# Expert tiles of a one-core MoE kernel: gate and up projections computed in turned form, with the weights staged by a VectorE copy

## The reference

```python
scores = sigmoid(h @ gate_w.T)                  # 32 experts, grouped choice, 8 of them per token
g = silu(einsum('th,eih->tei', h, w_gate))      # I = 128, H = 256
u = einsum('th,eih->tei', h, w_up)
routed = einsum('tei,ehi->th', g * u * combine[:, :, None], w_down)
shared = silu(h @ sh_gate.T) * (h @ sh_up.T) @ sh_down.T
out = x + routed + shared
```

## Time and profile before

| | |
|---|---|
| time, median of 3 runs (lowest to highest) | 616.68 us (615.47 to 618.01) |
| span of the profiled execution | 615.6 us |
| PE busy | 563.7 us (92%) |
| DVE busy | 411.4 us (67%) |
| ACT busy | 372.2 us (60%) |
| POOL busy | 363.9 us (59%) |

### The profile page before, as it was taken

The page is one execution under the profiler, slowest core; times in us unless marked ns, Lnnn a source line. Parts: engine busy times, 40 slices in busy tenths (PEclk is TensorE's granted clock), DMA queues, the critical chain, the costliest instruction groups (busy, mean ns, idle before and its releaser), DMA issues.

```text
span 615.6 us, 11543 instructions
## 1 busy us (share of the span) xinstructions
PE 563.7 (92%) x2669; PEld 419.9 (68%) x2669; DVE 411.4 (67%) x1587; ACT 372.2 (60%) x993; POOL 363.9 (59%) x414
## 2 busy tenths in 40 slices
PE   3989989889998898698998999999999999999995
PEld 2656557655766455455656888888888888888774
DVE  6965675986768987648776444445444444698778
ACT  1858888768776755552611666566566666676660
POOL 4334233622143377886777777777777777777730
PEclk9979999999999799899799999999999999999998
DMA  7999300000000023239364999876666667999956
GB/s 259 394 397 380 120 0 2 0 1 0 2 0 1 14 94 118 97 118 341 119 223 179 314 315 338 284 224 205 202 207 201 210 199 216 353 412 397 413 184 244
DMA packets 62063, 119.69 MB, mean 194 GB/s; under 512 B 8667, under 2 KB 45583, under 8 KB 59951
## 3 DMA queue, kind: packets, MB, share of 16 engines
q1 hardware_dynamic: 48079, 77.63, 37.5%
q0 software_dynamic: 13488, 41.04, 17.7%
q10 hardware_dynamic: 432, 0.29, 0.2%
HBM read 61.29 MB, written 57.64 MB: 193 GB/s over the span
## 4 chain that ended last, share of the span: by engine, by line
PE 70%; DVE 10%; POOL 6%; ACT 6%; DMA 5%; issue 3%; SPq 0%; DVEq 0%; POOLq 0%; ACTq 0%
PE ps L2027 20%; PE ps L2047 10%; PE ps L1689 6%; PE ps L1663 6%; PE ps L1678 5%; PE ps L1886 5%; PE ps L1702 5%; POOL xrows L609 4%; DMA hat<-yrows 3%; PE ps L2040 3%; PE ps L1649 2%; PE ps L1781 2%; PE ps L1787 2%; DVE tokrow L749 2%; DMA xs<-in_x 1%
## 5 line engine op out<-in xcount | busy, mean ns | idle before, releaser
L2027 PE MATMUL ps<-arena,mats 128*128 x636 | 164.2, 381 | 0.3 <-issue 0.3
L609 POOL DMA_INDIRECT xrows<-tokrow,place_of x128 | 125.8, 983 | 42.9 <-issue 37.2
L1274 DVE TENSOR_TENSOR mats<-ps,mats 128x128 f32<-128x128 f32 x159 | 46.3, 291 | 104.1 <-ACT mats L1460 99.8
L2027 PEld LDWEIGHTS ps<-arena,mats 128*128 128x128 f32 x636 | 108.5, 190 | 9.3 <-issue 0.8
L2047 PE MATMUL ps<-arena,mats 128*128 x318 | 95.7, 383 | 1.0 <-DVE mats L1281 1.0
L1460 ACT ACTIVATE mats<-ps 128x128 f32<-128x128 f32 x159 | 44.1, 277 | 57.0 <-PE ps L2027 57.0
L1453 ACT COPY mats<-ps 128x256 f32<-128x256 f32 x159 | 57.9, 364 | 11.8 <-PE ps L1886 11.8
L1402 ACT ACTIVATE hat<-tokrow,shift,rstd 128x256 f32<-128x256 f32 x96 | 49.7, 590 | 14.1 <-POOL shift L540 14.1
L1394 ACT ACTIVATE hat<-tokrow,total 128x256 f32<-128x256 f32 x96 | 47.5, 499 | 17.0 <-DVE tokrow L814 10.3
L2047 PEld LDWEIGHTS ps<-arena,mats 128*128 128x128 f32 x318 | 48.0, 191 | 13.5 <-issue 1.9
L545 POOL TENSOR_SCALAR var_eps<-variance 128x4 f32<-128x4 f32 x24 | 6.4, 266 | 83.5 <-ACT hat L1394 83.2
(11 more groups left out here) (239 smaller groups left out, 1136.4 us busy)
## 6 DMA issues: line engine op xcount, KB each, us to landing
hat<-xrows SPq DMA_DIRECT2D x81, 160.0 KB
rows<-xrows SPq DMA_DIRECT2D x78, 160.0 KB
arena<-in_experts SPq DMA_DIRECT2D x4, 1920.0 KB, 18.9
xrows<-padrow SPq DMA_DIRECT2D x32, 160.0 KB
hat<-yrows SPq DMA_DIRECT2D x5, 1024.0 KB, 9.0
tokrow<-yrows SPq DMA_DIRECT2D x5, 1024.0 KB, 9.6
hatT<-yrows SPq DMA_DIRECT2D x5, 1024.0 KB, 9.3
xrows<-padrow SPq DMA_DIRECT2D x1, 4960.0 KB
```

The source lines that it names most:

```text
L609: gp.indirect_dma_start(out=xrows[:, :], out_offset=bass.IndirectOffsetOnAxis(ap=place_of[:, g, k:k + 1], axis=0), in_=tokrow[:, g, :], in ...
L2027: mm = te.matmul(bank(6 + u)[:, 0:2 * I], turned_row[u][:, dc * P:(dc + 1) * P], arena[:, dc * D:(E - 1) * WCOL + (dc + 1) * D][:, bass.ds ...
```

## The change

Gate and up are computed with the roles exchanged: the weights are stationary and the turned rows are moving, so that each product comes out turned (expert columns on the partitions, tokens along the row). A stationary operand at an offset from a register is not used; VectorE copies the 512 columns of gate and up of the tile's expert to one of two fixed places (`stage_weights`, line 1288 of the changed kernel), two tiles ahead. The turn of the product and the copy after it are gone; `down` comes one step earlier in the loops of PE and ACT. The gate half is signalled on its own. Some result buffers lie in other places, and the last one of the first round (tile 47) may be written only after the last dispatch has landed.

```diff
-        ybuf += [part(mats[:, i, :, :], D, D) for i in range(3)]
+        ybuf += [part(mats[:, 0, :, :], D, D)]
...
+        ybuf += [part(tokrow[:, :, :], T * ROW + TOPK * D + i * D, D) for i in range(2)]
...
-        silu, act, actT = ([part(mats[:, j, :, :], i * I, I) for i in range(2)] for j in range(3))
+        silu = [part(mats[:, 0, :, :], i * I, I) for i in range(2)]
+        act = [part(buffer[:, :, :], ROWBUFS // 2 * ROW, I) for buffer in (hat, rows)]
+        staged = [part(mats[:, 1 + i, :, :], 0, DC, D) for i in range(2)]
...
             def product(s):
                 u = s % 2
                 ve.wait_ge(silu_done, s + 1)
-                if s >= 2:
-                    ve.wait_ge(act_turned, s - 1)
-                ve.tensor_tensor(act[u], bank(6 + u)[:, I:2 * I], silu[u], ALU.mult).then_inc(act_ready, 1)
-
-            def copy_act(s):
-                u = s % 2
-                ve.wait_ge(act_turned, s + 1)
+                ve.wait_ge(gate_up_done, s + 1)
                 if s >= 2:
                     ve.wait_ge(down_done, s - 1)
-                ve.tensor_copy(actT[u], bank(u)[:, 0:I]).then_inc(actT_ready, 1)
+                ve.tensor_tensor(act[u], bank(u)[:, 0:I], silu[u], ALU.mult).then_inc(act_ready, 1)
+
+            def stage_weights(s, at):
+
+                if s >= 2:
+                    ve.wait_ge(gate_up_done, s - 1)
+                ve.tensor_copy(staged[s % 2].rearrange("p c d -> p (c d)"),
+                               arena[:, 0:(E - 1) * WCOL + DC * D][:, bass.ds(at, DC * D)]).then_inc(staged_ready, 1)
...
+            ve.wait_ge(weights_in, 16 * 6)
+            for n in range(-2, TILES + 2):
                 if 1 <= n <= TILES:
                     product(n - 1)
+                s = n + 2
+                if s < TILES:
...
+                    stage_weights(s, base[s % 4])
...
             def copy_out(n):
                 ac.wait_ge(down_done, n + 1)
+                if n == YFIRST - 1:
+                    ac.wait_ge(dispatched[3], 16 * TQ * TOPK)
...
-                for dc in range(DC):
-                    mm = te.matmul(bank(6 + u)[:, 0:2 * I], turned_row[u][:, dc * P:(dc + 1) * P],
-                                   arena[:, dc * D:(E - 1) * WCOL + (dc + 1) * D][:, bass.ds(at, 2 * I)],
-                                   start=dc == 0, stop=dc == DC - 1)
-                mm.then_inc(gate_up_done, 1)
+                for half in range(2):
+                    if s == 0 and half == 1:
+                        te.wait_ge(sh_added, 2 * NB)
+                    for dc in range(DC):
+                        mm = te.matmul(bank((6 if half == 0 else 0) + u)[:, 0:I], staged[u][:, dc, half * I:(half + 1) * I],
+                                       turned_row[u][:, dc * P:(dc + 1) * P], start=dc == 0, stop=dc == DC - 1)
+                    mm.then_inc(gate_done if half == 0 else gate_up_done, 1)
...
-                te.transpose(bank(u)[:, 0:I], act[u], ident[:, :]).then_inc(act_turned, 1)
```

More of the change, by code:

```diff
@@ L236, in y_place @@
                 return YHELD + (n - YLATE) % (YBUFS - YHELD)
-            return n if n < YFIRST else (n - YFIRST) % YBUFS
+            if n >= YFIRST:
+                return (n - YFIRST) % YBUFS
+            if n == YFIRST - 1:
+                return YBUFS - 1
+            return n if n < YBUFS - 2 else n + 2
         def y_last(n):
@@ L1336, in vector_program @@
             starts = [tiles_from(phase) for phase in range(3)]
-            for n in range(TILES + 2):
+            ve.wait_ge(weights_in, 16 * 6)
+            for n in range(-2, TILES + 2):
                 if 1 <= n <= TILES:
                     product(n - 1)
+                s = n + 2
+                if s < TILES:
+                    if s in starts:
+                        ve.wait_ge(tables_ready, 3 * (starts.index(s) + 1))
+                    if s % 4 == 0:
+                        _, base = nc.values_load_multi_w_load_instructions(
+                            weight_at[0:1, s:s + 4], engines=[mybir.EngineType.DVE], min_val=0,
+                            max_val=(E - 1) * WCOL, skip_runtime_bounds_check_because="no more than the last expert")
+                    stage_weights(s, base[s % 4])
+                if n < 0:
+                    continue
                 m = n // GROUP
@@ L1456, in gate @@
                 u = s % 2
[L1457 removed]
+                ac.wait_ge(gate_done, s + 1)
                 if s >= 2:
@@ L1623, in scalar_program @@
             ac.wait_ge(weighed, 2 * NB)
-            for n in range(TILES + 3):
+            for n in range(TILES + 2):
                 if n < TILES:
```

45 lines of the change are left out of this document (13 added, 32 removed).

## The result

| | kernel before | changed kernel |
|---|---|---|
| time, median (lowest to highest), 4 runs each, same chip | 616.08 us (614.92 to 618.01) | 631.75 us (631.46 to 634.22) |
| ratio, with its 95% interval | | 1.0256 (1.0227 to 1.0285) |
| span of the profiled execution | 615.6 us | 633.0 us |

The change makes the kernel 2.6% slower. The forecast had the sign (slower, chance 0.60) and about a quarter of the size: it said 621.0 us, 4.3 over the 616.68 that it started from, and 631.75 lies above its range. The profiled execution of the changed kernel is the longest of its four: the others have spans of 630.1 to 630.7 us, so its times at the end are some 2.5 us later than those of a median run.

A forecast was written before the change was run, and what follows sets the result against it. GpSimd's gapless DMA queue was taken as the bound: span 615.6 + 4.9 of copy delays = 620.5, less about 0.6 for a quieter last landing, plus 1.1 from span to median, gives 621.0 us (+0.7%); range 616.0 to 629.0.

The forecast's parts named there:

- The reading of what bounds the kernel: Tile loop: GpSimd's queue of 222 indirect DMAs has no gap in 286 us, and its end is on the path.
- worth nothing: TensorE in the tile loop: 1.54 us a tile, 13.5 us less over the loop, but no gain on the path.
- The copy: VectorE's staging copy of 512 columns from SBUF to SBUF, one a tile: 0.44 us each.
- Its delays of GpSimd: Tile loop: staging copies across DMA starts lengthen GpSimd's DMAs, 0.031 us a copy, 4.9 us for 157.
- The forecast's formula: Mean DMA delay from a VectorE operation of duration d at random phase: (d - 0.16)^2 / 2 / 1.265.
- Rival 1: Staging copy doesn't disturb the start of a GpSimd DMA, or does so for less: 616 to 617.5 us; chance 0.24.
- Rival 3: Every copy overlapping a DMA holds it for all its remaining time: 26 us, 642; chance 0.08 with milder forms.
- Tile 47's wait: ScalarE, and TensorE behind it, stand 6 to 10 us for the last dispatch; GpSimd has its backlog and loses nothing.
- From tile 120: Late tile loop: 1.7 to 1.8 us a tile, tile 152's result at 589, before GpSimd reaches it at 595.4.
- Rival 2: Tile chain becomes the end, VectorE above 1.95 us a tile from tile 120: 624, up to 629 us; chance 0.12.
- The end. Unchanged, 25 us: After the last scatter's issue: landing, reads and sums stay as before, 25 us.
- I am wrong if ... GpSimd waits for ScalarE before it: Sign against the forecast: last scatter before 592 us, or GpSimd waiting for ScalarE before that scatter.

The follow-up runs named there:

- nocopy_2: Changed kernel with staging copies for tiles 0 and 1 only, all later tiles using those weights: 614.78 us, ratio 0.9976 to the kernel before.
- late_only: Changed kernel with the staging copy left out from tile 2 to tile 115 and kept from 116 on: 628.41 us, ratio 1.0236 to the kernel before.

## Why the prediction was wrong

**The reading of what bounds the kernel** was right: GpSimd's queue. nocopy_2 makes tiles faster and gains nothing (by then the last tile's own way to the end is as long), and useless early copies, which lengthen GpSimd's DMAs by 4.3 us more than before, cost 5 to 6 us.

**TensorE**, 0.112 us a matmul and 1.54 us a tile, "worth nothing": right (1.546; 0.9976).

**The copy**, 0.44 us: right (0.427). **Its delays of GpSimd**, 4.9 us: right in rule, and in size as long as GpSimd has no gap. Up to 520 us the DMAs of the changed kernel are 4.4 us longer, against 0.8 before, and the rule gives 3.6 for 116 copies. After 520 us they are 2.5 us longer, against 4.6 before, and nothing of it reaches the end. The forecast's formula took 0.16 us off where its rule says 0.13, without a reason; with 0.13 it gives 6.0. The trace has one: 16 copies that began less than 0.04 us before a DMA did not lengthen it. Rival 1, that a copy with one input doesn't disturb, is out: see the 1.21 us DMA above. Rival 3 is out as well. The Trainium skill (SBUF — State Buffer, the box on the "DVE blocks DMA" trap) says that such a copy makes GpSimd stand until it ends. By the traces it does so only for a DMA that starts during the copy, less 0.13 us. A copy that starts inside a DMA hardly holds it; this pair of the changed kernel shows who gives way more:

```profile
559.31 1.01 POOL L711 DMA_INDIRECT yrows<-tokrow,mats  x1 [0.30 <-ACT tokrow L1488]
...
559.92 0.63 DVE L1288 COPY mats<-arena 128x512 f32 x1
```

The copy has 0.63 us instead of 0.43, and the DMA 1.01.

**Tile 47's wait**: 5.0 us instead of 6 to 10, and no effect that the medians show. "GpSimd has its backlog: nothing" holds only while GpSimd is the path; once the tile chain is, what it lost at tile 47 can count, up to 5 us in single traces. That the early tiles would run at 1.54 us was wrong: 1.60, for VectorE's own turns.

**The step that failed is "From tile 120 ... I expect 1.7 to 1.8 ... 529 + 33 x 1.75 + 2 = 589 ... Just covered".** Measured: 606.2, 17 us later, and three things went wrong in it.

1. *The rate*, 32 x (2.04 - 1.75) = 9 us. The forecast added the copy's 0.44 us to VectorE's busy 1.25 us a tile and left a little for waits. VectorE indeed is busy only 1.75 to 1.79 us a tile (30.77 and 29.98 of 35 us, times 2.04). What it left out is the order: in front of the copy stands a wait for products that TensorE makes in the same turn, behind it stand the sums, and behind them the product that TensorE waits for. The order listing ahead of the prediction shows that wait in so many words. The forecast held the offsets' load hidden "as long as VectorE waits there", but never asked what is queued behind that wait once the sums begin.
2. *The start*, 541.0 - 535.9 = 5 us. Early tiles at 1.60 us and 5.0 us at tile 47 were to cancel against the faster tiles, and didn't.
3. *The base*, 3 us. The turn with the first sum was put at 529, and a result one turn and 2 us later, which gives 533 for tile 120. In the kernel before that turn starts at 530.4 and the result is there at 535.9.

Rival 2 ("the tile chain becomes the end", chance 0.12) is what happened, at its very rate: it named 2.05 us a tile. But it inherited errors 2 and 3, so it gave 624 instead of 632.

**"The end. Unchanged, 25 us"** failed too. From the last scatter to the end it is 633.0 - 606.5 = 26.5 us, and no longer by the same road. VectorE is in the loop until 617.5, though the first of the last reads had landed at 613.8. (The last read waits for the last tile too, which ended late_only.) With a late loop the end is not "last scatter plus 25".

The signs that the forecast set for itself were sharp enough: "I am wrong if ... GpSimd waits for ScalarE before it". It does, from tile 130 on.

No version here is faster than the kernel before. The staging copies, with their waits and loads, are the whole loss, and with GpSimd's queue as the bound their best case was a tie.

## What to carry to other kernels

When a change puts a wait into an engine's program, list what is queued behind it in every stage of the loop, and who waits for that; busy time by tile tells nothing of it (the wait ahead of the copy cost 0.17 us a tile, the 0.43 us of copying itself 0.12 to 0.15). When two paths finish together, as GpSimd's queue and the tile chain did here, work out both to the end with their real starting points, as a cost on the one that is covered today counts once it has passed the other: the early copies brought tile 120's result 7.4 us later, which delayed no scatter while GpSimd was behind, and did delay the last ones.

## What was not expected of the hardware

- A float32 copy within SBUF counts for GpSimd's indirect DMAs like an operation with two inputs in SBUF: a DMA that starts while it runs grows by the rest of it, less 0.13 us (1.21 instead of 0.96 us). In the changed kernel's tile loop this holds to 0.01 us for the 29 copies that had more than 0.13 us left and had begun more than 0.04 us before the DMA. The 16 that began less than 0.04 us before the DMA cost it nothing and took 0.46 to 0.50 us.
- A copy that starts inside a DMA costs it little: the 57 DMAs in the changed kernel's loop with such a copy and no VectorE operation across their start took 0.96 to 1.02 us, median 0.960. The copy is itself stretched, to 0.66 us at most.
- A VectorE operation that reads PSUM, or a TENSOR_REDUCE, across the start of a DMA lengthened none by 0.01 us or more: six and nine cases in the changed kernel with more than 0.13 us left.
- A copy of 128 x 512 in SBUF takes 0.427 us on VectorE and 0.618 us on ScalarE. A copy of 128 x 8 still takes 0.16 to 0.37 us on VectorE, 0.17 in the median.
- The chips differ: the same kernel before takes 614 to 616 us on some and 718 to 723 on two. On one of these each engine does much less between 340 and 480 us (TensorE 74.7 us of work instead of 134.4), and in four stretches of 1.6 to 4.2 us there none of the four engines works. There GpSimd isn't the bound, and ratios differ: the kernel without copies had 1.016 on it and 0.998 on another chip.
